# Moving the second sort group's slots, its products, one norm and two tag steps between tiles of a software-pipelined pass

## The reference, cut to what matters

```python
# layer 0
messages = concat([x[src], edge_attr_64], -1) @ W_message
agg = segment_sum(messages, dst)
h = layer_norm(relu(agg) + x)
x1 = layernorm(x + layer_norm(x + mlp_skip(h)))       # three dense layers
# layer 1, with tgt = src and nbr = dst
h = lrelu(x1 @ w_W + w_b);  edge_h = lrelu(edge_attr_128 @ ew_W + ew_b)
e = concat([h[tgt], h[nbr], edge_h], -1) @ a_W + a_b
out = segment_sum(softmax_over_tgt(e) * h[nbr], tgt)
return layernorm(x1 + lrelu(out))
```

## Time and profile before

| | us |
|---|---|
| median of 3 runs (lowest, highest) | 6549.06 (6542.9, 6576.24) |
| the profiled execution | 6568.37 |
| its span, first to last instruction | 6566.5 |
| the loop of passes, from the first `hb` to the last | 197.8 to 3773.0 |
| mean TensorE clock granted, share of full | 0.818 |

### The profile page before, as it was taken

One profiled execution on the slowest core, in us unless ns is written; L12 is line 12 of the kernel. 1 busy time (PEld: TensorE's weight loads), 2 busy tenths in 40 slices (PEclk: granted clock), 3 DMA queues, 4 the chain that ended last, 5 costly groups with the idle time before them and its releaser, 6 DMA issues. The chain is left out here.

```text
span 6566.5 us, 86603 instructions
## 1 busy us (share of the span) xinstructions
PE 4225.2 (64%) x18560; PEld 3124.8 (48%) x18561; DVE 3554.9 (54%) x11327; ACT 1857.5 (28%) x5457; POOL 3533.8 (54%) x3615
## 2 busy tenths in 40 slices
PE   4677767777777777777777745555555555555555
PEld 3455545555554555555555534444444444444444
DVE  8455556555555655655655644454444444444444
ACT  0122222222222222222222213333333333333333
POOL 0554555555455555555555525566666566666664
PEclk8788888888888888888888877788777787777777
DMA  2444444444444444444444622333333333533332
GB/s 73 112 120 113 114 114 121 115 116 119 116 115 118 117 116 120 120 119 118 118 112 119 117 73 80 89 92 94 92 91 92 87 93 90 87 95 92 89 93 71
DMA packets 546642, 679.47 MB, mean 103 GB/s; under 512 B 341874, under 2 KB 379360, under 8 KB 546222
## 3 DMA queue, kind: packets, MB, share of 16 engines
q0 software_dynamic: 172416, 464.26, 26.6%
q1 hardware_dynamic: 359216, 201.09, 11.7%
q10 hardware_dynamic: 14976, 13.69, 0.6%
HBM read 648.41 MB, written 29.43 MB: 103 GB/s over the span
## 5 line engine op out<-in xcount | busy, mean ns | idle before, releaser
L662 POOL DMA_INDIRECT rows<-in_x,picked x1785 | 1789.6, 1003 | 1683.0 <-ACT picked L854 1130.6
L1570 POOL DMA_INDIRECT nbr<-nodetab,nbr_idx x1700 | 1617.7, 952 | 1026.5 <-issue 469.8
L693 PE MATMUL bank<-w_edge,feats 128*128 128x258 f32 x3264 | 1127.8, 436 | 620.1 <-ACT bank L835 335.4
L708 PE MATMUL bank<-rows,hot 128*128 128x320 f32 x3570 | 1356.9, 479 | 48.3 <-issue 45.1
L1600 PE MATMUL bank<-nbr,w 128*128 128x258 f32 x3400 | 1044.2, 471 | 280.9 <-issue 135.6
L835 ACT COPY bank<-b_edge 128x258 f32<-128x258 f32 x1635 | 611.3, 379 | 2136.4 <-DVE unused L1063 1554.2
L1063 DVE SCALAR_TENSOR_TENSOR unused<-bank,a_relu 128x258 bf16<-128x258 f32 x1632 | 687.4, 423 | 969.3 <-remote 530.3
L1600 PEld LDWEIGHTS bank<-nbr,w 128*128 128x128 f32 x3400 | 802.6, 243 | 479.0 <-issue 168.1
L693 PEld LDWEIGHTS bank<-w_edge,feats 128*128 128x128 f32 x3264 | 627.0, 214 | 841.9 <-ACT bank L835 381.1
L1632 ACT ACTIVATE w<-off,logit 128x128 f32<-128x128 bf16 x1700 | 525.8, 391 | 1501.6 <-DVE logit L1703 1171.7
L708 PEld LDWEIGHTS bank<-rows,hot 128*128 128x128 f32 x3570 | 760.3, 214 | 267.9 <-issue 114.2
(11 more groups left out here) (320 smaller groups left out, 4056.9 us busy)
## 6 DMA issues: line engine op xcount, KB each, us to landing
feats<-in_edge SPq DMA_DIRECT2D x408, 256.0 KB
rows<-in_edge SPq DMA_DIRECT2D x255, 128.0 KB, 2.6
rows<-in_x,picked POOLq DMA_INDIRECT x1785
nbr<-nodetab,nbr_idx POOLq DMA_INDIRECT x1700
rows<-in_edge SPq DMA_DIRECT2D x153, 160.0 KB
nodetab<-tab ACTq DMA_DIRECT2D x52, 129.0 KB
x_blk<-in_x SPq DMA_DIRECT2D x52, 128.0 KB
x_rows<-u_n ACTq DMA_DIRECT2D x52, 128.0 KB
```

The source lines that it names most:

```text
L662: pool.indirect_dma_start(out=rows[:, STARTS[j] + s, 0:D], out_offset=None, in_=a["x"], in_offset=bass.IndirectOffsetOnAxis(ap=picked[j][: ...
L693: mm(y, feats[:, f0 * P:(f0 + 1) * P], w_edge[:], start=False, stop=True, skip_group_check=True).then_inc(o["y_ready"], 1)
L708: ins = mm(S_PS, hot[j % HR][:, s - STARTS[j], :], rows[:, s, :], start=(s == 0), stop=(s == SA - 1), skip_group_check=True)
L1570: pool.indirect_dma_start(out=nbr[:, TOFF[u] + k, :], out_offset=None, in_=nodetab, in_offset=bass.IndirectOffsetOnAxis(ap=nbr_idx[u][:, k ...
```

## The change

- DVE makes slots 2 and 3 (group u=1) at tiles 6 and 9 of the next pass instead of at 26 and 28 of this one; slots 0 and 1 are now made at 18 and 28 instead of at 18 and 21. So tiles 21 and 26 lose a slot, tiles 6 and 9 gain one.
- PE multiplies group u=1 one tile later (13 to 16), with a wait of its own for slots 2 and 3; pack, turn and keep of that group follow one tile later on ACT and PE.
- `out_norm` ends after its two norm steps; the addition of x and the statistics are a step of their own at tile 24.
- The one-hot of batch 0 moves from tile 24 to 25, and the last key tag from 25 to 26.
- Ahead of the loop `rank_two` is set to zero, behind it two slot instructions are added.

```diff
 def sort(w, u, tiles, last=False):
     if tiles[0] == 0:
+        pe.wait_ge(o["slot_ready"], w * 4 + (u * 2 + 2))
         if u == 0:
-            pe.wait_ge(o["slot_ready"], w * 4 + 4)
             pe.wait_ge(o["tagged_ready"], w + 1)
...
-        for u, first in enumerate((4, 12)):                      # PE: products
+        for u, first in enumerate((4, 13)):
-        if kk in (9, 17):                                        # PE: turn_rows
+        if kk in (9, 18):
-        if kk in (8, 16):                                        # ACT: pack
+        if kk in (8, 17):
-        if kk in (10, 18):                                       # ACT: keep_rows
+        if kk in (10, 19):
...
     step(d, v.scalar_tensor_tensor(u2[:], u2[:], rstd[:, 0:1], row["out_bias"], ALU.mult, ALU.add))
+
+def add_x_again(d):                                              # DVE, tile 24
     step(d, v.tensor_tensor(u2[:], u2[:], x_blk[:], ALU.add))
     measure(d)
...
-        if kk in (18, 21, 26, 28):
-            slots(p, (18, 21, 26, 28).index(kk))
-        if kk in (17, 20, 25):
-            tag_keys(p, (17, 20, 25).index(kk))
+        if kk in (6, 9):
+            slots(p, 2 + (6, 9).index(kk))
+        if kk in (18, 28):
+            slots(p, (18, 28).index(kk))
+        if kk in (17, 20, 26):
+            tag_keys(p, (17, 20, 26).index(kk))
         if kk in hot_at:
             one_hot(p, hot_at[kk])
+        if kk == 25:
+            one_hot(p + 1, 0)
...
-        if kk == 24:
-            one_hot(p + 1, 0)
...
-dve.sem_inc(o["slot_ready"], 4)
+link(v.memset(rank_two[:], 0.0))
+dve.sem_inc(o["slot_ready"], 2)
```

More of the change, by code:

```diff
@@ L801, in body @@
                             triangle(p)
-                        if kk in (9, 17):
-                            turn_rows(p, (9, 17).index(kk))
+                        if kk in (9, 18):
+                            turn_rows(p, (9, 18).index(kk))
                         if kk in node:
@@ L923, in body @@
                             pick(p + 1, pick_at[kk], tile)
-                        if kk in (8, 16):
-                            pack(p, (8, 16).index(kk))
-                        if kk in (10, 18):
-                            keep_rows(p, (10, 18).index(kk))
+                        if kk in (8, 17):
+                            pack(p, (8, 17).index(kk))
+                        if kk in (10, 19):
+                            keep_rows(p, (10, 19).index(kk))
                         if kk == 10:
@@ L1164, in table @@
                     assert count[0] == NDV, count[0]
-                node = {5: add_x, 7: first_norm, 12: residual(0), 15: residual(1), 18: residual(2), 21: out_sum, 23: out_norm, 25: last_norm,
-                        30: table}
+                node = {5: add_x, 7: first_norm, 12: residual(0), 15: residual(1), 18: residual(2), 21: out_sum, 23: out_norm,
+                        24: add_x_again, 25: last_norm, 30: table}
                 SUM_KK = [SUM_AT[s] for s in STARTS]
@@ L1246, in _ @@
                     tag_logits(n, m)
+                for m in (2, 3):
+                    slots(n, m)
                 count[0] = 0
```

## The result

The changed kernel takes **6638.6 us** (median of 12 runs, 6596.6 to 6654.6) against 6572.1 us of before measured beside it (12 runs, 6542.9 to 6594.6): ratio **1.0099, 95% interval 1.0079 to 1.0119**. It is slower by 1%, where the forecast was 6556 (+0.1%) and the range ended at 6590. The forecast stood on 6549.1, the median of three runs; from the 12 runs' median its +7 us would have been 6579, and the measured change is +66.5 us. The profiled run has a span of 6633.0 us, against 6566.5: 66.5 us more.

A forecast was written before the change was run, and what follows sets the result against it. The loop was taken as bound by waits, with PE's updates held from DVE during POOL's DMA runs. Terms 0.26 + 0.43 - 0.35 - 0.23 = +0.11 us a pass, with the tail +7 us, gave 6556 us; range 6508 to 6590.

The forecast's parts named there:

- The model of three runs, three stretches and the hold: Each pass: three POOL DMA runs hold PE's updates from DVE until about 2 us after; stretches between cost full time.
- Slot at tile 9: Free for DVE, but delays the first gather of POOL's first run: +0.43 us a pass, bounds 0 and 0.47.
- Slot at tile 28: Falls behind the third run's third gather, which is no longer lengthened: -0.35 us a pass, by a margin of 0.05 us.
- Rival 2: Slower: the reliefs at tiles 28 and 23 to 26 fail, the costs stay; +40 us, 6596 us, chance 0.17.
- The other gathers of the first run ... +-0.1: Coming 0.43 us later, they meet other DVE instructions; taken at nothing, within +-0.1.
- Slot at tile 6: On the path between third run's release and the pick at tile 9: +0.26 us a pass, bounds 0 and 0.61.
- Tiles 23 to 26: Stretch ahead of the third run, priced by the last edge stopped: -0.23 us a pass, bounds -0.7 and +0.6.
- Rival 1: Faster: first dense layer's update slips through before the hold, second stretch 1.0 us shorter; -50 us, 6505 us, chance 0.2.
- sign of being wrong altogether: The tile at which a hold stops DVE moves for most passes, which can shift a stretch by several us.

The follow-up runs named there:

- g2: Before's code with DVE gated after POOL's three runs at edges 16, 24 and 1, where the changed kernel stops; +2.6 us a pass against g1.
- g3: The changed code with DVE gated at its own stops, edges 16, 24 and 1; +0.7 us a pass against g1.
- h1: Before with only the norm split over two tiles, the one-hot at tile 25 and the last tag at 26; 0.9972 on a chip with the hold.
- g1: Before's code with DVE waiting at edges 14, 23 and 4 until POOL's run has landed; 3.3 us a pass longer than before on the result's chip.
- h2: The changed kernel without norm split, one-hot and tag moves, and its slot of tile 9 at tile 10; 0.9961 of before on a chip with the hold.
- g4: The changed code with before's gates, at edges 14, 23 and 4; +4.0 us a pass against g1.
- e1: Before with only the second group's products, pack, turn and keep one tile later; 0.9999 on a chip without the hold.
- f1: The kernel of e1 in the next batch, against before; 1.0002 on a chip without the hold.
- i1: The kernel of e1 again, against before; 0.9998 on a chip without the hold.
- j1: The kernel of e1 again, against before; 1.0001 on a chip without the hold.
- k1: The kernel of e1 again, against before; 1.0004 on a chip without the hold.

## Why the prediction was wrong, step by step

- **The model of three runs, three stretches and the hold** held. All of the change is in the stretches and in the gathers that lengthen a run, and the table above is the model with its prices measured.
- **Slot at tile 9**: forecast +0.43, and the first gather of run 1 takes 1.38 us on average instead of 0.95, in 46 of 46 passes: +0.43. By the Trainium skill (SBUF — State Buffer, section "SBUF: two separate sides") a VectorE instruction with two SBUF inputs, as the slot is, contends with a GpSimd instruction that reads SBUF, and whichever starts first keeps the other waiting to its end. The trace agrees for the gather that starts second (1.38 instead of 0.95 us), if its reading of the picked indices is what contends, which no run here separates. It disagrees for the other order. Here the gather at 2020.75 takes its 0.95, and the slot that starts 0.12 behind it its usual 0.69:

```profile
2020.75 0.95 POOL L662 DMA_INDIRECT rows<-in_x,picked  x1 [0.30 <-ACT picked L854]
2020.87 0.69 DVE L1032 TENSOR_TENSOR slot<-one_up,rank_two 128x1024 bf16<-128x1024 bf16 x1
```

- **Slot at tile 28**: forecast -0.35, measured -0.37 (the third gather of run 3 took 1.32 on average, now 0.95, with none above 1.2). Rival 2, whose condition was that this margin of 0.05 us fails, did not come.
- **"The other gathers of the first run ... +-0.1"** was too small. Run 1 is 0.75 us longer, of which 0.43 is the first gather. DVE no longer stands still at tile 12 and works beside more of the gathers.
- **Slot at tile 6**: forecast +0.26. With equal stops the nearest pair is g2 and g3 at edge 1, 16.7 and 17.1 us, +0.4, within the bounds 0 and 0.61.
- **Tiles 23 to 26**: the prediction counted edge 23 in 23 of 46 passes and edge 24 in 7. By the rule used here they are 17 and 11 of 45, with which its own sum gives -0.08 instead of -0.23. Its price was -0.73 with the stop at 23; before and changed kernel differ there by -0.5, before and h1 by -0.8. With the stop at 24 the price was +0.61; the table has -0.6 and -0.1, and +0.4 between g2 and g3. This stretch came out 0.80 us shorter, and how much of it is the stops and how much the moves is not separated.
- **Rival 1** came true in its event and not in its chance, its size or its reason. It said that the update of the first dense layer, due earlier behind the moved products, slips through, and gave that 0.2 because "edge 14 is bound to the run's end in the other 46". It happened in all passes. The 5 passes that spoke for it are those with POOL's pause (1.62 us idle inside the run), which the prediction did not read. Its reason, the due time, is not borne out, since in 7 passes of g1 an update due at +4.03 to +4.26 is still held. The due time given, 4.1 us, was off too (4.49), because the hit makes the first gather longer and does not move its start. It gave 2.6 us ahead of run 2 where 1.0 was expected, since the stop went to edge 16 and not to 15.
- **The step that failed** is that the sum held the stops of the hold fixed, and the third run's above all. It priced the slot of tile 6 and the rest of the stretch ahead of run 1 with DVE stopped at edges 3 and 4, and put a move of that stop at nothing, though the prediction's last lines say of it: "that can shift a stretch by several us, and nothing in the trace of before tells its sign". Its own sign of being wrong altogether, that the tile at which a hold stops DVE moves for most passes, came true. The third run's stop moved to 0 and 1 in 38 of 45 passes, and the stretch ahead of run 1 grew by 4.2 us where the sum had 0.26. This made the sign of the whole. Only a part of the price could have been read: before's 6 passes with the stop at edge 1 wait 13.8 us instead of 11.3. With 13.8 for edge 0 as well, the changed kernel's stops would have given +1.9 us ahead of run 1, and less than the 2.6 us won ahead of run 2, so that the sum would still have come out as a gain.
- **The range** ended at 6590, since both rivals moved one stretch at a time.

What stays open: why the third stop moves. The rows show what goes with it. PE's hidden layer, on which DVE works ahead of edge 31, ends 5.0 us into run 3 in the changed kernel and is seen at 7.2 (medians); in before it is 4.1 and 5.1, in h1 4.6 and 4.7, in h2 5.4 and 5.7. In the 21 passes that stop at edge 0 the update is late by 2.3 us, in g4's 41 by 3.7, in before's 17 that stop at edge 4 by 0.3. So at edge 0 the hold catches the hidden layer's own update, and what makes it do so is not shown. A late due time alone is not it, as h2 shows, and a short stretch ahead of run 3 is not either, as g4 shows, which has 8.2 us there and edge 0 for its stop. Open too are what lets the first layer's update through, and what distinguishes the chips.

## What to carry to other kernels

Where an engine is stopped by something that begins and ends by itself (a hold, a throttle, a burst of another queue), price the stop and not the instruction: list for each pass at which instruction the stop falls and how long what follows takes, because one update that slips through, or is caught, is worth several us either way (+4.2 and -2.6 us a pass here). Passes of the same trace in which the stop falls otherwise are a first price list, though here a short one. Before they are read as near misses, look at what else differs in them: here it was a pause of POOL in every ninth pass. Measure on more than one chip before a change of 1% is kept or thrown away: here the same edit is 0.991 on one and 1.010 on another.

## What the runs showed of the hardware

- The same program takes 5010 to 5017 us on some chips and 6429 to 6632 on others, with the same busy times of DVE and POOL in the loop. The granted clock of TensorE over the loop is 0.97 on the first kind and 0.86 on the second, but most of the loop's 1043 us is DVE's waiting for late updates (819 us from 300 to 3700 us, 505 of them ahead of edges), of which e1 has none, with POOL issuing indirect DMAs all the time.
- On chips with the hold the late updates do not trickle in. The first layer's, due at +5.04 us in nearly all passes of before, is seen at +5.08 (5 passes) or at 9.3 to 10.1 (40 passes), and at nothing between; due at +4.49 in the changed kernel it is seen at +4.54 or at 5.20 to 5.26 in all passes but two, in which it is due and seen sooner. On the chip of h1 the late ones come at 7.1 to 9.9.
- An earlier due time does not by itself get an update through: due at +4.03 to +4.26 in 7 passes of g1 it is seen at +7.2 to +9.3, due at +4.49 in the changed kernel at +5.3 at the latest.
- In every ninth pass (12, 21, 30, 39, 48) of before, h1, g1 and g2, POOL idles 1.6 us behind its first indirect DMA of the pass instead of 0.30, and in all of these passes the first layer's update is seen by +5.4.
- A gather whose record starts up to 0.13 us behind the start of a 0.69 us slot instruction takes 1.38 to 1.42 us instead of 0.95. A slot that starts 0.12 or 0.19 us behind a gather takes its 0.69 us, and the gather its 0.95.
- Where there is no hold, the place of the products is worth nothing (e1, f1, i1, j1, k1: 0.9998 to 1.0004).
